# A decoder layer's recurrence on TensorE: half products in 64 by 32 tiles, k's projection in two parts, a loop of six pairs

## What is computed

```python
q = (x @ Wq).reshape(b, s, H, HD)          # H = 16 heads of HD = 16
k = (x @ Wk).reshape(b, s, H, HD)
v = (x @ Wv).reshape(b, s, H, HD)
fg = jax.nn.sigmoid(x @ Wf + bf).reshape(b, s, H, HD)
...
def step(state, inp):
    qt, kt, vt, gt = inp
    state = state * gt[..., None] + vt[..., None] * kt[..., None, :]
    out_t = jnp.einsum('bhij,bhj->bhi', state, qt)
    return (state, out_t)
state0 = jnp.zeros((b, H, HD, HD), x.dtype)
_, outs = jax.lax.scan(step, state0, (qs, ks_, vs, gs))
```

## Time and profile before

| | us |
|---|---|
| median of 3 runs | 2437.17 |
| lowest, highest | 2437.17, 2446.89 |
| the profiled execution | 2458.95 |
| its span, first to last instruction | 2457.2 |
| recurrence on TensorE, of that span | 70 to 938 |

### The profile page before, as it was taken

The page is one execution under the profiler, slowest core; times in us unless marked ns, Lnnn a source line. Parts: engine busy times, 40 slices in busy tenths (PEclk is TensorE's granted clock), DMA queues, the critical chain, the costliest instruction groups (busy, mean ns, idle before and its releaser), DMA issues. The chain is left out here.

```text
span 2457.2 us, 74676 instructions
## 1 busy us (share of the span) xinstructions
PE 2201.4 (90%) x30260; PEld 1498.7 (61%) x30260; DVE 1668.7 (68%) x3029; ACT 1134.1 (46%) x1874; POOL 271.6 (11%) x273
## 2 busy tenths in 40 slices
PE   1788888888889895999999999999699999999498
PEld 1466666666666664777777777777444444444387
DVE  5576676666666775666667676766455557987797
ACT  0343333333333342666666666666311117854365
POOL 0100000000000000111111111111000004433221
PEclk9799998998988997999999999999899999999799
DMA  2010000001000001101010101010000003459675
GB/s 85 14 29 21 24 26 20 21 22 27 21 21 23 26 16 48 39 28 38 26 38 26 38 26 38 26 38 13 1 0 0 0 0 138 200 197 360 242 261 173
DMA packets 78436, 146.95 MB, mean 60 GB/s; under 512 B 10131, under 2 KB 63638, under 8 KB 78230
## 3 DMA queue, kind: packets, MB, share of 16 engines
q1 hardware_dynamic: 78230, 143.70, 17.1%
HBM read 82.84 MB, written 60.82 MB: 58 GB/s over the span
## 5 line engine op out<-in xcount | busy, mean ns | idle before, releaser
L1273 PE MATMUL ff_bank<-ff_xq,w_uh 128*128 (+1 forms) x1536 | 457.7, 380 | 6.8 <-ACT ff_whole L1380 6.8
L1273 PE MATMUL ff_bank<-ff_xq,w_ul 128*128 (+1 forms) x768 | 291.3, 379 | 0.0
L1273 PEld LDWEIGHTS ff_bank<-ff_xq,w_uh 128*128 128x128 f16 x1536 | 149.7, 98 | 187.4 <-issue 11.4
L586 ACT ACTIVATE x<-rec_e 128x512 f32<-128x512 f32 x192 | 112.1, 596 | 275.0 <-PE rec_e L475 275.0
L487 PE MATMUL rec_x<-x 32*32 32x64 f32 x8192 | 160.1, 230 | 60.3 <-issue 54.9
L1575 DVE TENSOR_REDUCE ff_top<-ff_bank 128x512 f32 (+1 forms) x192 | 132.8, 692 | 116.5 <-PE ff_bank L1273 116.4
L487 PEld LDWEIGHTS rec_x<-x 32*32 32x32 f32 x8192 | 138.8, 114 | 94.1 <-issue 93.9
L1380 ACT ACTIVATE ff_whole<-ff_bank,ff_coef 128x512 int16<-128x512 f32 x192 | 120.6, 682 | 117.6 <-DVE ff_out L1614 63.4
L686 DVE TENSOR_TENSOR rec_tmp<-rec_x,x 32x256 f32<-32x256 f32 (+1 forms) x192 | 80.8, 421 | 136.6 <-PE rec_x L512 68.5
L650 DVE TENSOR_TENSOR x<-rec_x,rec_until 128x512 f32<-128x512 f32 x256 | 158.7, 682 | 21.7 <-PE rec_x L459 21.7
L1062 DVE TENSOR_REDUCE mneg<-att_s 128x4 f32<-128x512 f32 x256 | 159.0, 684 | 5.5 <-PE att_s L878 4.6
(11 more groups left out here) (229 smaller groups left out, 4385.7 us busy)
## 6 DMA issues: line engine op xcount, KB each, us to landing
gate_scratch<-ff_out SPq DMA_DIRECT2D x28, 768.0 KB, 3.5
ff_in<-gate_scratch SPq DMA_DIRECT2D x28, 768.0 KB, 6.7
product_scratch<-ff_out SPq DMA_DIRECT2D x28, 768.0 KB, 6.0
ff_out<-product_scratch SPq DMA_DIRECT2D x28, 768.0 KB, 5.9
att_x<-in_x SPq DMA_DIRECT2D x32, 256.0 KB, 2.7
att_ctx<-in_ctx SPq DMA_DIRECT2D x32, 256.0 KB, 3.0
att_o<-rec_scratch SPq DMA_DIRECT2D x32, 256.0 KB, 3.7
out<-s_out SPq DMA_DIRECT2D x16, 512.0 KB, 3.3
```

What stands on the lines that cost most here:

```text
L1273: m = T.matmul(bank_[:], weights(wp, kc, a, c), tile[:, xp, kc], start=(i == 0), stop=(i == len(terms) - 1))
```

## The change

`across` gets the half `oc` as a parameter: it waits ahead of half 0 and signals behind half 1. `products` issues both halves for q, but only half 0 for k. Half 1 of k is issued in `pieces`, in turn 0, behind the first `inside`. `across_half` writes each 64 output columns as two tiles of 32, so its 32 matmuls on 64x64 tiles become 64 on tiles of 64 rows by 32 columns, from the same operands. TensorE's loop body holds six pairs in place of two, with 5 rounds in place of 15. The loops of the other engines stay as they were.

```diff
+    TURNS = 6
...
-                def across(p, i, bank_, b, done):
-                    pe.wait_ge(q["v_ready"], 2 * p + b + 1)
-                    for oc in range(KC):
-                        for kc in range(KC):
-                            m = T.matmul(bank_[:, oc * 2 * P:(oc + 1) * 2 * P], wr[:, kc, i, oc * P:(oc + 1) * P],
-                                         xT[:, kc], start=(kc == 0), stop=(kc == KC - 1))
-                    m.then_inc(done, 1)
+                def across(p, i, bank_, b, oc, done):
+                    if oc == 0:
+                        pe.wait_ge(q["v_ready"], 2 * p + b + 1)
+                    for kc in range(KC):
+                        m = T.matmul(bank_[:, oc * 2 * P:(oc + 1) * 2 * P], wr[:, kc, i, oc * P:(oc + 1) * P],
+                                     xT[:, kc], start=(kc == 0), stop=(kc == KC - 1))
+                    if oc == KC - 1:
+                        m.then_inc(done, 1)
...
-                            src, dst = halves[b], halves[1 - b]
-                            m = T.matmul(X[0][dst, at], mt[src, b, hd, dst], wa[src, 1, at], start=True, stop=True)
+                            src = halves[b]
+                            for dst in (rows(2 - 2 * b), rows(3 - 2 * b)):
+                                m = T.matmul(X[0][dst, at], mt[src, b, hd, dst], wa[src, 1, at], start=True, stop=True)
...
-                        across(p, 0, F[1], 0, q["q_made"])
-                        across(p, 1, F[0], 1, q["k_made"])
+                        across(p, 0, F[1], 0, 0, q["q_made"])
+                        across(p, 0, F[1], 0, 1, q["q_made"])
+                        across(p, 1, F[0], 1, 0, q["k_made"])
...
+                        if front and i == 0:
+                            across(p, 1, F[0], 1, 1, q["k_made"])
...
-                with pe.Fori(0, (NP - 2) // 2) as j:
-                    for u in range(2):
-                        p, s = 2 * j + 1 + u, (1 + u) % 2
-                        pieces(p, s, j + u, True, True, True)
+                with pe.Fori(0, (NP - 2) // TURNS) as j:
+                    for u in range(TURNS):
+                        p, s = TURNS * j + 1 + u, (1 + u) % 2
+                        pieces(p, s, TURNS // 2 * j + (1 + u) // 2, True, True, True)
                         products(p + 1, p, 1 - s, s, True, True)
```

## The result

The changed kernel takes 2480.37 us (median of 4 runs, 2470.13 to 2490.39) beside 2442.03 for the kernel before (2437.17 to 2455.88). The ratio is 1.0159, with a 95% interval of 1.0125 to 1.0193: it is slower by 30 to 47 us. The forecast was no change, 2443 us.

The account below looks back on a forecast made before the run. PE was taken to wait for its own program, in blocks of 256 instructions of 3.85 us. The terms -38 + 5 + 54 - 12 = +9, less another 3, left +6 us: 2443 us, within 2431 to 2455.

Parts of the forecast that it names:

- The reading: In the recurrence, PE waits for its own program, in blocks of 256 instructions of 3.85 us; 69 us of such waits.
- The edges: Behind the loop's branch: ten fewer at 3.8 us, -38; five worse covered, +5; more pairs like the second, -3 us.
- The half products: In the thin stretch: 128 more instructions a pair, half a block, +1.93 us each or +62 us; taken as +54.
- a reserve: Second pair's block with the half products: PE needs 0.5 us more than the block takes; counted in half of the pairs.
- rival 2: Recurrence: half clock in every pair, 15 more pairs paying 1.76 us, +26 us, 2469 us; chance 0.18.
- k's second half: Moved from thick to thin stretch, 0.9 us hidden in waits in 15 to 16 pairs; -14 to +6, taken as -12 us.
- +6: Whole kernel: the forecast's summed change in us, +9 by its terms less another 3 for six pairs more.
- Rival 1: Recurrence: blocks come faster in straight code, 3.68 us each, -25 to -30 us, 2415 us; chance 0.28.
- Rival 3: Half products: tiles of the same rows don't overlap, 32 ns each, 4.1 us for 128, 2457 us; chance 0.12.

Follow-up runs that it names:

- The kernel with one tile: The changed kernel with the second of each two 64x32 tiles left out of the half products (half of what they compute missing); 2403.69 us, ratio 0.9872.

## Why the prediction was wrong, point by point

**The reading was right.** The waits come at equal distances of 256 instructions in the changed kernel too. Between a wait ahead of the half products and the next ahead of the quarter products there are 3.9 us (25 cases, 3.3 to 4.3), where 3.7 to 4.0 was foretold. L504 has 39.0 us of idle time (30 or more), long waits stand among the first inside products behind the five branches only (1.6 to 2.0 us four times, 1.0 us behind the last), and the half products lie 9.9 ns apart (1.23 us for 124). In pairs without half clock the thin stretch has grown from 11.5 to 13.0 us on the mean, and the thick one has shrunk, from 12.27 in the earlier trace rows to 11.4 or 11.5 in nine of ten. PEclk of the recurrence is 0.91 (0.92). A list of signs that all come true doesn't make a sum right.

**The edges: right.** -38 + 5 - 3 = -36 was forecast, -43 (27 to 59) measured by the loop of six alone. But what the -43 is made of was not seen. Beside the waits, half of the time at half clock went: 123 us of the 30 pairs before, 58 with six alone.

**The half products: this step failed.** The sum took +54, from +62 less a reserve. Measured were +79 and +86 in the loop of six (some 18 either way) and +78 (some 9) without edges. The cause of the cost was right, its size was not. The term was sized as a block's time, at the clock that the trace of before showed: "If the blocks set the time, each pair pays 3.85 / 2". That part is not even full. A straight line fitted over the pairs (their length against their time at half clock) gives a pair without half clock 24.9 us with the tiles and 24.0 without: 0.9 us or 27 us in all, 1.4 us more of waits less 0.5 us of busy time, since the half products are shorter. The rest is clock. With six and k split 44 us of the 30 pairs ran at half clock, with the tiles 130. In each kernel of these loops, a microsecond at half clock goes with a pair 0.3 to 0.5 us longer, 0.53 and 0.47 in these two, and nearly all of that is in PE's busy time (0.45 and 0.40), not in its waits. By these lines the 44 us cost 24 and the 130 cost 61, so the tiles' half clock costs some 37 us, an estimate, and 27 + 37 is the 64 us by which the 30 pairs differ.

That waits ahead of the half products let the clock fall is what the order of time suggests. In the changed kernel's 30 pairs the clock falls 21 times, 11 of them with or behind a wait of 1.7 to 2.7 us there (2.69 us, then 0.42 in place of 0.27 above); with the half products whole it falls 11 times, never so. The kernel with one tile has no such wait, and 41 us at half clock. The other falls stand at waits elsewhere, and an experiment on the clock alone was not made, so how the cost divides between blocks and clock is worked out and not shown; that instructions that have to be fetched cause both is shown by the kernel with one tile and by the body of one pair, where the tiles gain.

**Why the trace of before misled.** In it, 23 of 30 pairs have half clock already, so there the tiles find little more to spoil: +35 alone in the loop of two, with no more time at half clock than before. The loop of six cleared the clock in 14 of those pairs, and the tiles took it back: -43 and +35 singly, +43 together. The prediction summed both parts from a trace in which neither had been made. Its rival 2 had the mechanism, half clock that follows a thin stretch, but priced it as a sign of its own, 15 pairs more beyond the number in the trace of before, not as something that part 1 removes and part 2 brings back. Its time, 2469, was the nearest, and PEclk under 0.90, which was to show it, never came: the mark was held against the kernel before (0.92) and not against the loop of six with the split (0.95), which nobody had seen.

**k's second half: mis-sized, of either sign.** -12 was forecast. Measured were +9 (1 to 17) alone, +3 in six and -5 with the tiles (some 22 and 12 either way), -13 (some 12 either way) with thirty written out, +7 and +10 in the body of one pair. Only the thirty pairs show a gain, and where nothing is waited for it seems to cost; why, and whether the two changes of tile form do it, was not tested. Added to six alone, it misses by 15 us, and the tiles by 25; with the 7 us by which the edges gave more, that is the 33 between +6 and +39.

**Rival 1** (faster blocks in straight code, 2415) fell: 3.9 us between such waits with six pairs, 3.8 with thirty (27 cases, 3.3 to 4.3). **Rival 3** (tiles of the same rows don't overlap, 32 ns) fell: 128 of them take 1.26 us, 9.8 ns apart. The Trainium skill (TensorE: Matmul & The Clock Gate, Part 3, What overlaps and what doesn't) allows a weight load to overlap a running matmul on another row group only; here two tiles in a row share their 64 rows, and the trace disagrees.

## What to carry over

Where an engine waits in the middle of a row of equal instructions at a fixed distance counted in instructions, it waits for its program: count the instructions of a loop's body before anything else, and make the body short enough to stay on the chip (here 1587 stayed and 1971 didn't, and 1107 gave 117 us), since until then an edit that trades one instruction for two cheaper ones pays for both. When a change has several parts that touch the same clock or the same wait, the trace of before prices only the first one; price the second on what the first leaves, and take a loss of clock as part of a wait's cost.

## What the runs showed of the hardware

A block of 256 instructions takes TensorE 3.8 to 3.9 us to get when it stands waiting, with thirty pairs in straight code as in a loop of six. A body over the limit doesn't miss a little: at 1971 instructions, some 10 packets a round came for a body that touches 9 blocks (44 packets in 200 us, at 46 us a round), so all of it is fetched again. And two matmuls on the same 64 rows and neighbouring columns follow each other in 10 ns (128 in 1.26 us), so that a 64x64 product cut in two tiles of 32 columns takes 20 ns in place of 32.
